# A transformer layer on one core: VectorE takes over the low parts of split queries and keys from GpSimd

## The chip, the cores and the metric

One Trainium2 chip, one core of it. The metric is the device time of one execution in microseconds; three runs of the kernel before gave a median of 1078.43 (1077.81 to 1080.08). The engines' short names in the profile are PE (TensorE), DVE (VectorE), ACT (ScalarE), POOL (GpSimd) and SP (SyncE).

## The reference, cut to what matters

Batch 8, sequence 1024, width 192, 12 heads of 16, hidden width 768, all float32.

```python
h = segm_table[seg] + pos + token_table[tok]
x = layernorm(h)
q, k, v = split(x @ qkv_weight.T)              # per head, 16 wide
q = layer_norm(q) * 16 ** -0.5                  # normalised over the 16
k = layer_norm(k)
h = h + softmax(q @ k.T) @ v @ proj_weight.T
x = layernorm(h)
xq = round(clip(x / mean(alpha_a1), -8, 7));  wq1 = round(clip(w1 / alpha_w1[:, None], -8, 7))
x1 = clip(gelu(xq @ wq1.T * alpha_w1 * mean(alpha_a1) + b1), -10, 10)
hq = round(clip(x1 / mean(alpha_a2), -8, 7)); wq2 = round(clip(w2 / alpha_w2[:, None], -8, 7))
h = h + hq @ wq2.T * alpha_w2 * mean(alpha_a2) + b2
```

## The kernel before

The 8 sequences are cut into 16 halves of 512 tokens, each of four tiles of 128 (TH = 4). The kernel runs 18 half-steps as a software pipeline: in half-step s TensorE, ScalarE and VectorE do the attention of half s, the first norm, the QKV projection and the split of queries and keys of half s + 2, the projection and the FFN's first part of half s - 1, and the FFN's end of half s - 2. Before half-step 0 a start does the work of the first halves ("half -1", "half -2" below are the passes labelled s = -1 and -2). No loop of the hardware is used; every instruction is written out.

Attention is done in 24 units a half-step (UNITS): a unit is a group of 4 heads against one tile of 128 keys. Per unit TensorE multiplies the scores (`scores`, L1073), ScalarE takes exp in two passes (`exps`, L645), and two units later TensorE multiplies by the values (`heads`, L1093), over a PSUM bank that VectorE copies out once in 8 units (`head_outputs`, L796, word `o`).

Between the units stands the other work, in an order written out by hand: PLAN (L77) has one line for a unit, START_PLAN (L128) is the same for the start and half-step 0. Every engine walks through the same list and does its part of each word, in this order; an engine's queue is never reordered. The capital words are jobs: TensorE fills one of three PSUM banks (`job`, L1097), then VectorE (or ScalarE, where START_PLAN has the small letter) copies it out (`job_result`, L819); job n + 3 in the list waits for the copy of job n. The words that matter here: B the query and key projection, r the sums of squares on VectorE, S the reciprocal roots on VectorE (`qk_roots`, a chain of 12 small linked instructions), n0 to n3 the split of one tile each (`split_qk`), D and E the transposes of the stacked queries and keys, C the values, x0 to x5 the quantising of gelu's output (`quantise_gelu`, L812, three instructions each: L815, L816, L817), Y the FFN's second matmul (L1171). Y0 waits for the last of the six `hq`. The end of a half-step's list is `S0 n0 / n1 o / D0 x0 E0 C1 / n2 C2 D1 / E1 n3 / D2 x1 / D3 E2 x2 / E3 x3 x4 / x5 C3`, and the next one begins with `o / Y0 Y1 Y2 F0 ...`.

Queries and keys go to TensorE as float16 pairs, a high part and a rest (low part), four copies of 16 columns for each head: q as high, high, low, low and k as high, low, high, low. `split_qk` makes them: one product (`sq`, L778) scales the tile by its root, then two casts write the high parts of q and k (L783). The low parts, float32 minus high, are two subtractions that GpSimd does (`split_low`, L564), each 128 x 384. `sq` and `stack` have two buffers each (t % 2). TensorE's D and E wait for `stack_ready`, which GpSimd raises. In half -2 VectorE does the low part of k itself (L789), beside GpSimd's low part of q.

GpSimd's queue in a half-step: `add_result` (the bias and the residual of the FFN, it waits for the last Y copy of VectorE), four gathers of segment rows and four of token rows for a half three ahead, the squares of four tiles (L553, for r), and at the end `split_low`. In the start the gathers of token rows of halves 2 and 3 stand behind `split_low(-2)` and `split_low(-1)`. SP issues the loads of positions and the stores.

On VectorE an instruction that reads what the one ahead wrote is linked to it by a semaphore (`link`, L670): the queue waits for its end. Instructions without a link overlap by a little.

Of the kernel before, what the change touches and what calls it, by code (L numbers as in the profile page):

```python
# [25 lines left out]
ALU = mybir.AluOpType  # L26
# [4 lines left out]
B, SEQ = 8, 1024  # L31
C = 192
H, D = 12, 16
HID = 768
TB = SEQ // P
TH = TB // 2
# [163 lines left out]
def job_half(kind, s):  # L200
    return s + LAG[kind]


def job_runs(kind, s0):
    return s0 == 1 if kind == "W" else 0 <= job_half(kind, s0) < HALVES
# [26 lines left out]
def layer(nc, x_tok, x_seg, tok_table, seg_table, w_qkv, w_proj, w1, b1, aw1, aa1, w2, b2, aw2, aa2,  # L232
          pos, out):
    ctx = ExitStack()
    with ctx:
# [3 lines left out]
        def sem(name):  # L239
            return ctx.enter_context(nc.semaphore(name))  # L240
# [31 lines left out]
        def squares_at(half0, t):  # L272
# [70 lines left out]
            sem(n) for n in ("hot_ready", "hot_mm", "hot_out", "rows_mm", "rows_added"))  # L343
        w_mm, scale_ready, high_weights, warm_ready = (
            sem(n) for n in ("w_mm", "scale_ready", "high_weights", "warm_ready"))
        hn_first, low_k_ready, squared_act = sem("hn_first"), sem("low_k_ready"), sem("squared_act")
        idx_ready, ident_ready = sem("idx_ready"), sem("ident_ready")
        pool_step, dve_step = sem("pool_step"), sem("dve_step")
        weights_ready, proj_ready = sem("weights_ready"), sem("proj_ready")
# [3 lines left out]
            sem(n) for n in ("hn_ready", "stack_ready", "xq_ready", "hq_ready"))  # L353
        scores_mm, exp_done, heads_mm, heads_out = (
            sem(n) for n in ("scores_mm", "exp_done", "heads_mm", "heads_out"))
        squared, summed, high_ready = sem("squared"), sem("summed"), sem("high_ready")
        out_ready, stored = sem("out_ready"), sem("stored")
        job_mm = {k: sem(f"{k}_mm") for k in PER_HALF}
        job_out = {k: sem(f"{k}_out") for k in PER_HALF}
# [1 line left out]
        def nth(half, t, per):  # L361

            return half * per + (t + 1)
# [56 lines left out]
        def stack_parts(t):  # L420

            for n, (high, low) in enumerate(((slice(0, 2), slice(2, 4)), (slice(0, 4, 2), slice(1, 4, 2)))):
                src = sq[:, t % 2, n * C:(n + 1) * C].rearrange("p (h d) -> p h d", d=D)
                src = src.unsqueeze(2).broadcast_to([P, H, 2, D])
                yield stack[:, t % 2, n, :, high, :], stack[:, t % 2, n, :, low, :], src
# [66 lines left out]
        def _(pool):  # L492
# [51 lines left out]
            def square(s0, s):  # L544
                if not job_runs("B", s0):
                    return
                half = job_half("B", s)
                for t in range(TH):

                    pool.wait_ge(job_out["B"], nth(half, t, TH))  # L550
                    if job_half("B", s0) > 2 or t >= 2:
                        pool.wait_ge(summed, half * TH + (t - 1))
                    nc.gpsimd.tensor_tensor(sq[:, t % 2], qk[:, t], qk[:, t], ALU.mult).then_inc(squared, 1)  # L553

            def split_low(s0, s):
                if not job_runs("D", s0):
                    return
                for t in range(TH):

                    pool.wait_ge(high_ready, nth(job_half("D", s), t, TH))  # L560
                    parts_ = list(stack_parts(t))

                    for high, low, src in parts_ if s0 > -2 else parts_[:1]:
                        last = nc.gpsimd.tensor_tensor(low, src, high, ALU.subtract)  # L564
                    last.then_inc(stack_ready, 1)

            def add_result(s0, s):
                if not job_runs("Y", s0):
# [11 lines left out]
            def one(s0, s, b):  # L580

                add_result(s0, s)
                ahead = s0 + GATHER_AHEAD
                if FIRST_GATHERED <= ahead < HALVES:
                    add_segments(ahead)
                    add_tokens(ahead)
                square(s0, s)
                split_low(s0, s)

            pool.wait_ge(idx_ready, 3)  # L590
            add_segments(2)
            add_segments(3)
            split_low(-2, -2)
            add_tokens(2)
            split_low(-1, -1)
            add_tokens(3)
            halfsteps(one)

# [68 lines left out]
        def _(dve):  # L667
# [9 lines left out]
            tt = nc.vector.tensor_tensor  # L677
# [93 lines left out]
            def split_qk(s0, s, t):  # L771

                half, h0 = job_half("D", s), job_half("D", s0)
                g = lambda a: a.rearrange("p (g d) -> p g d", d=D)
                if TH * h0 + t >= 2:

                    dve.wait_ge(stack_ready, half * TH + (t - 1))
                link(tt(g(sq[:, t % 2]), g(qk_at(h0, t)), rq[:, t, 0:GROUPS].unsqueeze(2).broadcast_to([P, GROUPS, D]), ALU.mult))  # L778
                if TH * h0 + t >= 2:

                    dve.wait_ge(job_mm["E"], half * TH + (t - 1))
                for high, low, src in stack_parts(t):
                    last = nc.vector.tensor_copy(high, src)  # L783

                last.then_inc(high_ready, 1)
                if s0 == -2:

                    dve.wait_ge(high_ready, t + 1)
                    tt(low, src, high, ALU.subtract).then_inc(low_k_ready, 1)  # L789

            def head_outputs(s0, s, p):

# [213 lines left out]
        def _(pe):  # L1006
# [90 lines left out]
            def job(s0, s, kind, t):  # L1097
# [27 lines left out]
                        last = mm(ps[:, 0:hi - lo], partsT[:, t, m], w, start=(n == 0), stop=(n == len(passes) - 1))  # L1125
                if kind in "DE":
                    pe.wait_ge(stack_ready, nth(half, t, TH))
                    if s0 == -2 and kind == "E":
                        pe.wait_ge(low_k_ready, t + 1)
                    for i in range(H // 2):  # L1130
                        src = stack[:, t % 2, "DE".index(kind), 2 * i:2 * i + 2].rearrange("p h a d -> p (h a d)")
                        last = nc.tensor.transpose(bank16((kind, t), s0, F16)[:, i * P:(i + 1) * P], src, ident_h[:])  # L1132
# [94 lines left out]
```

## Time and profile before

| | |
|---|---|
| median of three runs | 1078.43 us |
| the profiled execution | 1076.59 us |
| its span | 1074.8 us |
| mean granted TensorE clock | 0.977 of full speed |
| GpSimd's subtractions L564 | 124, 120.6 us busy |
| VectorE's casts L783 | 128, 58.7 us busy |

The busy share of an engine says how full it is over the whole span, not whether it holds the others up. The chain of waits says that: it is followed back from the last instruction, at each step to what released it. In the timeline, several instructions of one line that follow each other are one row ("x2"), from the first's start to the last's end; a number in brackets is the time that the engine was idle ahead of it, and who released it.

### The profile page before, as it was taken

How to read it: one execution, taken by the hardware profiler on the slowest of the kernel's cores; microseconds unless marked ns; L12 is line 12 of the kernel's file. 1: busy time of each engine (PE TensorE's matmuls, PEld its weight loads, DVE VectorE, ACT ScalarE, POOL GpSimd, SP SyncE). 2: the span in 40 equal slices, each digit the busy share in tenths (PEclk: the TensorE clock that was granted, in tenths of full speed). 3: DMA queues.
4: the chain of work that ended last, by engine and by line, in shares of the span. 5: the costliest groups of instructions: out<-in, count | busy, mean ns of one | idle time of the engine just before them, and what ended most of it. 6: DMA issues, size and time to landing. Idle time of an engine off the chain costs nothing.

```text
span 1074.8 us, 19548 instructions
## 1 busy us (share of the span) xinstructions
PE 978.3 (91%) x7571; PEld 387.7 (36%) x7571; DVE 814.1 (76%) x2318; ACT 867.7 (81%) x937; POOL 415.6 (39%) x347
## 2 busy tenths in 40 slices
PE   5599999999999999999999999999999999989873
PEld 4333434334343433334342433434243343413131
DVE  5978869698786969788686968878696978715265
ACT  1387798897979888898979889797988889798951
POOL 6554513536344452644444353534445314101011
PEclk9799999999999999999999999999999999989995
DMA  7510200303011030203112040201102000000000
GB/s 161 127 20 12 31 1 1 45 2 70 5 31 16 17 59 1 45 1 62 14 23 23 1 75 2 39 7 30 16 10 37 1 16 1 16 1 16 1 15 16
DMA packets 25329, 28.61 MB, mean 27 GB/s; under 512 B 4979, under 2 KB 21622, under 8 KB 25238
## 3 DMA queue, kind: packets, MB, share of 16 engines
q0 software_dynamic: 16896, 11.80, 9.3%
q1 hardware_dynamic: 8192, 15.55, 4.8%
q8 instruction: 61, 1.00, 0.4%
q14 instruction: 30, 0.25, 0.1%
q10 hardware_dynamic: 150, 0.01, 0.0%
HBM read 21.06 MB, written 6.29 MB: 25 GB/s over the span
## 4 chain that ended last, share of the span: by engine, by line
PE 40%; ACT 29%; DVE 24%; issue 3%; POOL 3%; POOLq 0%; DMA 0%; DVEq 0%
ACT probs L645 22%; PE ps_o L1093 12%; PE ps_s L1073 8%; PE ps_j L1117 4%; ACT gelu L639 4%; PE ps_j L1171 3%; POOL stack L564 3%; PE ps_j L1125 2%; PE ps_j L1132 2%; PE ps_j L1138 2%; ACT L639 2%; PE ps_j L1157 2%; ACT L645 2%; PE ps_j L1142 2%; DVE hn L734 2%
## 5 line engine op out<-in xcount | busy, mean ns | idle before, releaser
L645 ACT ACTIVATE probs<-ps_s 128x1024 f32<-128x1024 f32 x768 | 736.5, 1023 | 126.0 <-PE ps_s L1073 121.5
L1093 PE MATMUL ps_o<-probs,v_sb 128*32 128x512 f32 x3072 | 394.9, 605 | 0.2 <-DVE o_sb L796 0.2
L1073 PE MATMUL ps_s<-qT,kT 64*128 64x512 f16 x1536 | 264.1, 384 | 35.0 <-ACT probs L645 24.5
L564 POOL TENSOR_TENSOR stack<-sq,stack 128x384 f16<-128x384 f32 x124 | 120.6, 993 | 161.6 <-DVE stack L783 161.6
L1073 PEld LDWEIGHTS ps_s<-qT,kT 64*128 64x128 f16 x1536 | 61.4, 93 | 299.8 <-ACT probs L645 273.8
L573 POOL TENSOR_TENSOR y_sb<-y_sb,b_row 128x768 f32<-128x768 f32 x16 | 29.0, 1815 | 277.8 <-DVE y_sb L868 277.8
L497 POOL DMA_INDIRECT h_all<-in_L_tok_token_table,idx x60 | 96.9, 1614 | 59.1 <-DMA h_all<-in_L_tok_segm_table,idx 40.8
L1093 PEld LDWEIGHTS ps_o<-probs,v_sb 128*32 128x32 f32 x3072 | 69.1, 109 | 123.7 <-issue 115.6
L553 POOL TENSOR_TENSOR sq<-qk 128x384 f32<-128x384 f32 x56 | 46.2, 826 | 139.5 <-DVE qk L831 139.5
L497 POOL DMA_INDIRECT h_all<-in_L_tok_segm_table,idx x56 | 87.2, 1557 | 15.2 <-issue 13.7
L639 ACT ACTIVATE gelu<-ps_j,b_sb,s_sb 128x512 f32<-128x512 f32 x96 | 69.9, 773 | 26.1 <-PE ps_j L1157 25.1
L1132 PE MATMUL ps_j<-ident_h,stack 128*128 128x128 f16 x768 | 61.3, 225 | 12.3 <-POOL stack L564 10.8
L831 DVE TENSOR_SCALAR qk<-ps_j,w_back 128x384 f32<-128x384 f32 x56 | 34.6, 618 | 48.6 <-PE ps_j L1125 48.5
L1125 PE MATMUL ps_j<-wh,partsT 128*128 128x384 f16 (+1 forms) x384 | 70.4, 293 | 1.1 <-ACT partsT L626 0.7
L796 DVE COPY o_sb<-ps_o 128x512 f32<-128x512 f32 x48 | 32.7, 681 | 47.7 <-PE ps_o L1093 47.7
L1132 PEld LDWEIGHTS ps_j<-ident_h,stack 128*128 128x128 f16 x768 | 45.6, 100 | 50.7 <-issue 39.8
L815 DVE TENSOR_SCALAR gelu<-gelu,ia,qlo 128x512 f32<-128x512 f32 x96 | 61.8, 643 | 2.0 <-ACT gelu L639 2.0
L1157 PE MATMUL ps_j<-xqT,w1T 96*128 96x512 bf16 x192 | 58.4, 402 | 4.1 <-ACT gelu L639 2.5
L783 DVE CAST stack<-sq 128x384 f16<-128x384 f32 x128 | 58.7, 500 | 2.2
L816 DVE TENSOR_SCALAR gelu<-gelu,qhi 128x512 f32<-128x512 f32 x96 | 53.8, 560 | 3.4
L1125 PE MATMUL ps_j<-wl,partsT 128*128 128x192 f16 (+1 forms) x256 | 53.1, 290 | 0.0
L1117 PE MATMUL ps_j<-wpT,oT 96*128 96x192 f32 x256 | 48.7, 333 | 0.0
(148 smaller groups left out, 1089.3 us busy)
## 6 DMA issues: line engine op xcount, KB each, us to landing
out<-h_all SPq DMA_DIRECT2D x16, 384.0 KB, 2.4
h_all<-in_positions SPq DMA_DIRECT2D x7, 768.0 KB, 5.1
gelu<-in_L_ffn_w SPq DMA_DIRECT2D x2, 576.0 KB, 11.7
h_all<-in_L_tok_token_table,idx POOLq DMA_INDIRECT x60
h_all<-in_L_tok_segm_table,idx POOLq DMA_INDIRECT x56, 4.6
probs<-in_L_attn_qkv_weight SPq DMA_DIRECT2D x2, 432.0 KB, 5.4
h_all<-in_positions SPq DMA_DIRECT2D x2, 384.0 KB, 6.2
o_nat<-in_L_ffn_alpha_a SPq DMA_DIRECT2D x1, 384.0 KB, 5.0
```

Of the source, the lines that this page charges most:

```text
L497: nc.gpsimd.indirect_dma_start(out=h_tile(half, j), out_offset=None, in_=table, in_offset=bass.IndirectOffsetOnAxis(ap=idx[:, which, t:t + ...
L564: last = nc.gpsimd.tensor_tensor(low, src, high, ALU.subtract)
L639: nc.scalar.activation(gelu[:, j], bank(("X", j), s0), ACT.Gelu, bias=b1_sb[:, j:j + 1], scale=s1_sb[:, j:j + 1]).then_inc(job_out["X"], 1)
L645: nc.scalar.activation(probs[:, u % PROBS, 2 * pair:2 * pair + 2], ps_s[:, 2 * pair:2 * pair + 2], ACT.Exp, scale=SCORE_SCALE).then_inc(ex ...
L783: last = nc.vector.tensor_copy(high, src)
L815: link(ts(gelu[:, t], gelu[:, t], ia2[:], qlo[:], ALU.mult, ALU.max))
L1073: last = mm(ps_s[:, j], kT[rows, par, head // 2, m * P:(m + 1) * P], qT[rows, par, head // 2, nh * NQ:(nh + 1) * NQ], start=True, stop=True)
L1093: last = mm(ps_o[32 * j:32 * j + 2 * D, :], v_sb[:, par, m, (GH * group + j) * VE:(GH * group + j) * VE + 2 * D], probs[:, u % PROBS, j], ...
L1117: last = mm(ps[:, 0:C], oT[:, t, k], wpT[:, k], start=(k == 0), stop=(k == 1))
L1125: last = mm(ps[:, 0:hi - lo], partsT[:, t, m], w, start=(n == 0), stop=(n == len(passes) - 1))
L1132: last = nc.tensor.transpose(bank16((kind, t), s0, F16)[:, i * P:(i + 1) * P], src, ident_h[:])
L1157: last = mm(ps, w1T[:, k, t * P:(t + 1) * P], xqT[:, k], start=(k == 0), stop=(k == 1))
```

## The change

`split_low` goes from GpSimd. In `split_qk` VectorE links to its casts, then does the two subtractions of the tile and raises `stack_ready` itself, in every half. The semaphores `high_ready` and `low_k_ready` fall away. The squares of GpSimd for tiles 0 and 1 get a wait of their own on `stack_ready`, since the buffer `sq` is now read last by VectorE.

```diff
@@ -343,7 +343,7 @@
             sem(n) for n in ("hot_ready", "hot_mm", "hot_out", "rows_mm", "rows_added"))
         w_mm, scale_ready, high_weights, warm_ready = (
             sem(n) for n in ("w_mm", "scale_ready", "high_weights", "warm_ready"))
-        hn_first, low_k_ready, squared_act = sem("hn_first"), sem("low_k_ready"), sem("squared_act")
+        hn_first, squared_act = sem("hn_first"), sem("squared_act")
         idx_ready, ident_ready = sem("idx_ready"), sem("ident_ready")
         pool_step, dve_step = sem("pool_step"), sem("dve_step")
         weights_ready, proj_ready = sem("weights_ready"), sem("proj_ready")
@@ -353,7 +353,7 @@
             sem(n) for n in ("hn_ready", "stack_ready", "xq_ready", "hq_ready"))
         scores_mm, exp_done, heads_mm, heads_out = (
             sem(n) for n in ("scores_mm", "exp_done", "heads_mm", "heads_out"))
-        squared, summed, high_ready = sem("squared"), sem("summed"), sem("high_ready")
+        squared, summed = sem("squared"), sem("summed")
         out_ready, stored = sem("out_ready"), sem("stored")
         job_mm = {k: sem(f"{k}_mm") for k in PER_HALF}
         job_out = {k: sem(f"{k}_out") for k in PER_HALF}
@@ -550,19 +550,10 @@
                     pool.wait_ge(job_out["B"], nth(half, t, TH))
                     if job_half("B", s0) > 2 or t >= 2:
                         pool.wait_ge(summed, half * TH + (t - 1))
+                    if t < 2 and job_half("B", s0):
+
+                        pool.wait_ge(stack_ready, half * TH + (t - 1))
                     nc.gpsimd.tensor_tensor(sq[:, t % 2], qk[:, t], qk[:, t], ALU.mult).then_inc(squared, 1)
-
-            def split_low(s0, s):
-                if not job_runs("D", s0):
-                    return
-                for t in range(TH):
-
-                    pool.wait_ge(high_ready, nth(job_half("D", s), t, TH))
-                    parts_ = list(stack_parts(t))
-
-                    for high, low, src in parts_ if s0 > -2 else parts_[:1]:
-                        last = nc.gpsimd.tensor_tensor(low, src, high, ALU.subtract)
-                    last.then_inc(stack_ready, 1)
 
             def add_result(s0, s):
                 if not job_runs("Y", s0):
@@ -585,14 +576,11 @@
                     add_segments(ahead)
                     add_tokens(ahead)
                 square(s0, s)
-                split_low(s0, s)
 
             pool.wait_ge(idx_ready, 3)
             add_segments(2)
             add_segments(3)
-            split_low(-2, -2)
             add_tokens(2)
-            split_low(-1, -1)
             add_tokens(3)
             halfsteps(one)
 
@@ -779,14 +767,12 @@
                 if TH * h0 + t >= 2:
 
                     dve.wait_ge(job_mm["E"], half * TH + (t - 1))
+                for high, _, src in stack_parts(t):
+                    last = nc.vector.tensor_copy(high, src)
+                link(last)
                 for high, low, src in stack_parts(t):
-                    last = nc.vector.tensor_copy(high, src)
-
-                last.then_inc(high_ready, 1)
-                if s0 == -2:
-
-                    dve.wait_ge(high_ready, t + 1)
-                    tt(low, src, high, ALU.subtract).then_inc(low_k_ready, 1)
+                    last = tt(low, src, high, ALU.subtract)
+                last.then_inc(stack_ready, 1)
 
             def head_outputs(s0, s, p):
 
@@ -1125,8 +1111,6 @@
                         last = mm(ps[:, 0:hi - lo], partsT[:, t, m], w, start=(n == 0), stop=(n == len(passes) - 1))
                 if kind in "DE":
                     pe.wait_ge(stack_ready, nth(half, t, TH))
-                    if s0 == -2 and kind == "E":
-                        pe.wait_ge(low_k_ready, t + 1)
                     for i in range(H // 2):
                         src = stack[:, t % 2, "DE".index(kind), 2 * i:2 * i + 2].rearrange("p h a d -> p (h a d)")
                         last = nc.tensor.transpose(bank16((kind, t), s0, F16)[:, i * P:(i + 1) * P], src, ident_h[:])
```

## Rows read from the trace of the kernel before

**Rows 1.** Page, part 1: busy us, share of span, instructions

```profile
PE 978.3 (91%) x7571; PEld 387.7 (36%) x7571; DVE 814.1 (76%) x2318; ACT 867.7 (81%) x937; POOL 415.6 (39%) x347
```

**Rows 2.** Chain of waits, half-step 13: start us, us, what

```profile
907.66 1.81 POOL stack L564 x2
909.46 0.14 issue
909.60 0.50 PE ps_j L1132 x6
...
920.76 1.59 PE ps_j L1171 x18
```

**Rows 3.** Single lines, whole span: ns min/median/max, first and last start

```profile
L564 POOL TENSOR_TENSOR stack<-sq,stack x124: 910/922/1287, 42.4 to 911.5; 128x384 f16<-128x384 f32 x124
...
L789 DVE TENSOR_TENSOR stack<-sq,stack x4: 557/559/559, 42.4 to 49.7; 128x384 f16<-128x384 f32 x4
...
L778 DVE TENSOR_TENSOR sq<-qk,rq x60: 548/557/1159, 65.1 to 908.8; 128x384 f32<-128x384 f32 x60
...
L778 DVE TENSOR_TENSOR sq<-probs,rq x4: 557/762/1265, 41.1 to 48.2; 128x384 f32<-128x384 f32 x4
...
L815 DVE TENSOR_SCALAR gelu<-gelu,ia,qlo x96: 537/542/951, 165.1 to 1062.7; 128x512 f32<-128x512 f32 x96
...
L816 DVE TENSOR_SCALAR gelu<-gelu,qhi x96: 485/486/1033, 166.1 to 1063.3; 128x512 f32<-128x512 f32 x96
```

**Rows 4.** Timeline of VectorE, half-step 13: start us, us, instructions

```profile
899.43 0.63 DVE L783 CAST stack<-sq 128x384 f16<-128x384 f32 x2
899.98 0.55 DVE L778 TENSOR_TENSOR sq<-qk,rq 128x384 f32<-128x384 f32 x1
900.56 1.96 DVE L783 CAST stack<-sq 128x384 f16<-128x384 f32 x2
902.44 0.68 DVE L796 COPY o_sb<-ps_o 128x512 f32<-128x512 f32 x1
903.26 0.56 DVE L833 COPY qT<-ps_j 128x768 f16<-128x768 f16 x1
...
920.10 0.43 DVE L817 TENSOR_SCALAR hq<-gelu 128x512 bf16<-128x512 f32 x1
```

**Rows 5.** 13 stretches ahead of Y0, VectorE: L783, L815, L778, L816 in turn

```profile
sum 280.54, DVE 49.94; mean DVE 3.84
...
sum 280.54, DVE 52.02; mean DVE 4.00
...
sum 280.54, DVE 36.08; mean DVE 2.77
...
sum 280.54, DVE 44.71; mean DVE 3.44
```

**Rows 6.** Timeline of GpSimd, half-step 13

```profile
900.14 2.16 POOL L564 TENSOR_TENSOR stack<-sq,stack 128x384 f16<-128x384 f32 x2 [5.29 <-DVE stack L783]
...
923.69 1.81 POOL L573 TENSOR_TENSOR y_sb<-y_sb,b_row 128x768 f32<-128x768 f32 x1 [11.10 <-DVE y_sb L868]
```

**Rows 7.** Timeline of TensorE: first and last of 13 Y0

```profile
182.10 1.66 PE L1171 MATMUL ps_j<-w2T,hq 128*128 128x192 bf16 x18
...
920.70 1.66 PE L1171 MATMUL ps_j<-w2T,hq 128*128 128x192 bf16 x18
```

**Rows 8.** VectorE from 61 to 83 us: L778, then L783

```profile
61.00:83.00 22.00, 3.41 (x4) 1.00 0.09 12
...
61.00:83.00 22.00, 3.12 (x8) 1.00 0.09 12
```

**Rows 9.** Timelines of the start: TensorE, VectorE, TensorE

```profile
82.75 0.33 PE L1145 MATMUL ps_j<-ident_h,parts 128*128 128x128 f16 x3 [1.04 <-DVE parts L738]
...
100.99 0.56 DVE L833 COPY qT<-ps_j 128x768 f16<-128x768 f16 x1 [1.44 <-PE ps_j L1132]
...
120.13 0.84 PE L1138 MATMUL ps_j<-ident,o_sb 128*128 128x128 f32 x6 [1.38 <-DVE o_sb L800]
```

## The prediction

> **What bounds the kernel now.** I read the page's busy shares first. TensorE is busy 91% of the span, ScalarE 81%, VectorE 76%, GpSimd 39% [rows 1]. No single share decides, so I followed one half-step in the chain of waits, in order of time. There GpSimd appears once: the two low-part subtractions of the third tile, 1.81 us, and behind them six transposes of TensorE [rows 2]. That looks like a wait that the change removes. The chain then runs on TensorE to the second FFN matmul (job Y0, L1171) at 920.76. The question is who else has to be ready at Y0.
>
> Y0 waits for the last `hq` of `quantise_gelu`, on VectorE. That instruction starts at 920.10 and takes 0.43, so it ends at 920.53 [rows 4]. A wait of TensorE on another engine takes 0.14 to be seen (the "issue" piece at 909.46) [rows 2], so Y0 could start at 920.67; it starts at 920.70 [rows 7]. VectorE has 0.03 us of slack at Y0. The timeline shows the same gap of 0.17 +- 0.01 at all 13 Y0 from 182.10 to 920.70, 61.54 us apart [rows 7]. TensorE and VectorE arrive there together: whatever lengthens VectorE's queue between the roots (S0) and the last `hq` (x5) moves Y0.
>
> In that stretch VectorE never rests, but for one place: the copy L796 starts at 902.44 and takes 0.68; an instruction without a wait starts some 0.08 before the end of the one ahead (casts 899.43 + 0.63, next at 899.98), so the queue is free at 903.04 and the qT copy starts at 903.26 [rows 4]. Idle: 0.22 us.
>
> **The change part by part.** (1) Added to VectorE, per tile (4 in a half-step): a wait between casts and subtractions, and two subtractions. The casts now run to their end (0.63 instead of 0.55 in the queue) and the link costs 0.03, as between all linked instructions (the product of 899.98, 0.55 long, ends at 900.53 and its casts start at 900.56) [rows 4]: +0.11. The subtraction has been on VectorE four times, in the prologue, for the key half: 557 to 559 ns, even beside GpSimd's own [rows 3]; less the overlap of 0.08 that is 0.48 in the queue, two are 0.96. Sum 1.07 a tile, 4.28 a half-step. The query form (other stride on the low part) is not shown on VectorE: from above the bound is 1.16 us, what the product L778 takes at worst [rows 3] (beside GpSimd, which won't be busy), from below 0.35, the second cast of a pair (0.63 less the 0.28 after which it starts is about that; the cast has one input less). I take 0.56, the row of the same operation.
>
> (2) Removed from VectorE: the slowing by GpSimd's subtractions. The second tile's casts take 1.96 where the first tile's take 0.63, and GpSimd runs two subtractions from 900.14 to 902.30 beside them [rows 4, 6]. The sums per half-step over the 13 stretches [rows 5] against the median, undisturbed durations [rows 3]: casts 3.84 against 4 x 0.63, so 1.32; L815 4.00 against 6 x 0.542, 0.75; L778 2.77 against 4 x 0.557, 0.54; L816 3.44 against 6 x 0.486, 0.52. Together 3.13. Copies from PSUM are not slower beside GpSimd (qT 0.56) [rows 4] and give nothing.
>
> The Trainium skill ("SBUF — State Buffer", Who interferes with whom) gives a reason: the second pair of SBUF ports is locked for a whole instruction by GpSimd or by a VectorE cast, copy or tensor_scalar in its double rate, and a VectorE instruction with two SBUF inputs fights with GpSimd's reads. This rule speaks against the change in one point: the new subtractions have two SBUF inputs and would be exposed themselves, so with any GpSimd instruction left beside them the sum would be larger, by up to that instruction's length. GpSimd has none left there (it is idle for 5.29 us ahead of its first subtraction and for 11.10 behind its last) [rows 6], so the sum stays; in the prologue, the one place where the two run side by side, VectorE's stayed at 557 to 559 [rows 3] and the trace does not bear the rule out.
>
> (3) Net for VectorE up to the last `hq`: 4.28 - 3.13 = +1.15; the idle 0.22 and the slack 0.03 take their share: Y0 moves by 0.90 us. TensorE meanwhile gains: the third tile's parts are ready 0.03 + 1.04 behind the casts instead of 1.81 and a hand-over [rows 2], but VectorE comes to that tile 0.2 later (+1.07 twice, less 1.33 at the casts, 0.22 idle and 0.40 at the first slow L815); my estimate is that the transposes start 0.3 earlier. TensorE then waits at Y0, so the gain is lost. After Y0 the chain is on TensorE's own queue [rows 2], with no slack that the move could vanish in: scores, heads, the projection, then the norm. 13 x 0.90 = 11.7.
>
> (4) The start. In the stretch 61 to 83 (half -1) four tiles are split: +4.28; L778 sums to 3.41 against 4 x 0.557 (-1.18), the casts to 3.12 against 2.52 (-0.60) [rows 8]: +2.5. TensorE waits there for VectorE's `parts`, 1.04 us at 82.75 [rows 9], so it comes through whole. In half 0 the first tiles' part vanishes: VectorE waits 1.44 us for TensorE at 100.99 [rows 9], more than two tiles add with some slowing gone, and again ahead of the third. The fourth tile's 1.07 comes out: TensorE waits 1.38 for L800 behind it, at 120.13 [rows 9]. In half -2 one subtraction a tile is added, 4 x 0.48 = 1.9, against the slowing of the four products there (median 762 and worst 1265, against 557) [rows 3], which is 1.1, and of what comes behind them: +0.4. Together 4.0; its bounds are 0 (VectorE has gaps that I can't place) and 2 x 4.28 + 1.9, near 10.
>
> (5) GpSimd's queue: 124 subtractions of 0.92 us at best leave [rows 3]. Four token gathers each of halves 2 and 3, which stood behind them, are issued earlier; earlier can only help who reads them: 0. Squares wait in steady halves for VectorE's copy and will still: 0. The new wait (square of tile 0 or 1 on `stack_ready` of the previous half) asks for the third and fourth tile of the half before, split a half-step (61.54 us) less some 20 ahead of it: 0. `add_result` waits 11.10 us for VectorE's y_sb [rows 6], so an empty queue does not bring it forward; DMA issues behind it stay where they are relative to it: 0. Behind the new link on VectorE stands everything up to x5; that is the cost above.
>
> Sum: 11.7 + 4.0 = 15.7 us on the profiled run's 1076.59 (its span 1074.8 and 1.8 around it), so 1092.3. The median of the three runs is 1078.43, 1.84 above the profiled run; with the same distance 1094.1. I predict 1094 us, slower by 1.5%.
>
> **The rivals.** *Faster* (8%): the slack at Y0 is VectorE's and not a tie, or a subtraction is cheaper. Then what counts is the one GpSimd piece on the chain. It decides from the point where eight subtractions are 0.90 cheaper together, 0.45 us each instead of 0.56. TensorE then gets its third tile's transposes 0.3 earlier each half-step: 13 x 0.3 = 4, so 1074.5. For it: the 1.81 us in the chain; against: four rows within 2 ns.
>
> The Trainium skill ("GPSIMD Engine Reference", Engine selection) sends elementwise work on a tile to VectorE, GpSimd being about twice slower for two inputs; here it is 0.92 against 0.56, 1.65 times [rows 3]. By it the move pays; that is this rival, and what it leaves out is whose queue is full.
>
> *Absorbed* (9%): Y0 moves, but a ScalarE run later in the half-step hides it (exp passes fill 81% of the engine) [rows 1], and only the start's 4 us or less comes through: between 1078.4 and 1083, say 1081. Against it: the chain behind 920.76 is TensorE's, not ScalarE's [rows 2].
>
> *The slowing stays* (4%): slow casts are VectorE's own, not due to GpSimd. Then 4.28 - 0.25 = 4.0 passes 13 times, and at the start up to 10: some 60 us, 1138. Against it: slow instructions stand beside GpSimd's and only there.
>
> *The change relieves nothing* because GpSimd's next work moves into the stretch and slows VectorE again (2%): at most 3.13 x 13 = 41 us more, 1135. Nothing is ready for it: GpSimd's next piece waits 11.10 us [rows 6].
>
> **How the numbers follow.** My forecast has 77%. Its own range: 0.90 is a difference of 4.28 and 3.13, each good to some 0.25, so 0.55 to 1.25 a half-step, 13 times that is 7 to 16; the start 1.5 to 6: 1087 to 1100. For the 8 in 10 I reach down into the absorbed case, to 1080, and up to 1100. Less than 0.2% (2.2 us) can't be told from no change here. Faster by more than that: 0.07. Within: 0.06 (the rest of the first rival, the lower end of the absorbed one). Slower: 0.87.
>
> **What would show it.** In the changed kernel's profile: cast pairs of 0.63 in every tile, and L815, L816 without slow ones (step 2); pairs of subtractions on VectorE of 1.04 us from first start to last end (step 1); VectorE busy 814 + 124 x 0.56 less the slowing, near 840; GpSimd near 415.6 - 120.6 = 295; a half-step of 62.4 instead of 61.54, read between Y0 starts; TensorE idle at Y0 by 0.8 to 1.2 with VectorE's `hq` as releaser (step 3); TensorE's wait at 82.75 longer by 2.5 (step 4). If the half-step is 61.2 and the transposes' wait is all that changed, the rival of a faster kernel is right. If Y0 moves and the half-step does not grow, it was absorbed.

## The result: 1.55% slower, and the profile after

The changed kernel takes 1096.31 us (median of 4 runs, 1092.76 to 1097.26) against 1078.32 (4 runs) before: ratio 1.0155, 95% interval 1.0136 to 1.0175 (the quotient of the two medians is 1.0167). The forecast was 1094. The profiled execution took 1095.96, 19.4 more than that of the kernel before, of which the sum had named 15.7.

The page of the changed kernel answers to [rows 1]; behind it the row of the subtractions, now VectorE's, with the mean duration in ns:

```profile
PE 983.0 (90%) x7571; PEld 392.4 (36%) x7571; DVE 829.4 (76%) x2442; ACT 867.6 (79%) x937; POOL 294.4 (27%) x223
...
L774 DVE TENSOR_TENSOR stack<-sq,stack 128x384 f16<-128x384 f32 x128 | 65.7, 555 | 2.2
```

GpSimd lost 121.2 us of work, VectorE's busy time grew by 15.3 only: 124 subtractions were added, some 69 us. Of that 44.0 came back, because the products, the casts and the first two quantising instructions became shorter (together 216.3 before, 172.3 now); most of the rest is the overlap of some 0.08 between neighbours in the queue, which busy time counts once. The single lines of the changed kernel show it (ns min/median/max; product, cast, first and second quantising instruction), against [rows 3]:

```profile
L766 DVE TENSOR_TENSOR sq<-qk,rq x60: 546/549/561, 66.9 to 928.1; 128x384 f32<-128x384 f32 x60
...
L771 DVE CAST stack<-sq x128: 341/359/539, 42.1 to 929.0; 128x384 f16<-128x384 f32 x128
...
L801 DVE TENSOR_SCALAR gelu<-gelu,ia,qlo x96: 535/540/546, 174.7 to 1081.6; 128x512 f32<-128x512 f32 x96
...
L802 DVE TENSOR_SCALAR gelu<-gelu,qhi x96: 485/486/490, 175.3 to 1082.2; 128x512 f32<-128x512 f32 x96
```

The long ones are gone: the worst product was 1159, the worst L815 (now L801) 951. Still the kernel is slower. TensorE's timeline says where, at the first and the last of the 13 Y0 [rows 7]; the brackets are the time that TensorE was idle ahead, and for whom:

```profile
191.85 1.31 PE L1155 MATMUL ps_j<-w2T,hq 128*128 128x192 bf16 x14 [0.90 <-DVE hq L803]
...
939.58 1.65 PE L1155 MATMUL ps_j<-w2T,hq 128*128 128x192 bf16 x18 [0.91 <-DVE hq L803]
```

Three things are to be seen. The first Y0 is 9.75 us later than before (182.10), the last 18.88 (920.70), so 12 half-steps cost 9.13, 0.76 each (most are 62.3 to 62.4 long, 61.54 to 61.63 before). And at each Y0 TensorE now waits 0.90 for the last `hq`, where the kernel before shows no wait. Behind the last Y0 nothing more is lost up to the kernel's last FFN matmuls (1083.27 - 939.58 = 143.69, and 1064.39 - 920.70 = 143.69).

One half-step of VectorE in the changed kernel, against [rows 4]: tile 0's and tile 1's casts with the subtractions behind them, the copy L782, the qT copy, and the end of the queue.

```profile
668.54 0.63 DVE L771 CAST stack<-sq 128x384 f16<-128x384 f32 x2
...
670.16 0.55 DVE L766 TENSOR_TENSOR sq<-qk,rq 128x384 f32<-128x384 f32 x1
670.74 0.63 DVE L771 CAST stack<-sq 128x384 f16<-128x384 f32 x2
671.40 1.03 DVE L774 TENSOR_TENSOR stack<-sq,stack 128x384 f16<-128x384 f32 x2
672.35 0.68 DVE L782 COPY o_sb<-ps_o 128x512 f32<-128x512 f32 x1
672.95 0.55 DVE L819 COPY qT<-ps_j 128x768 f16<-128x768 f16 x1
...
689.99 0.43 DVE L803 TENSOR_SCALAR hq<-gelu 128x512 bf16<-128x512 f32 x1
```

From the first tile's casts to the second's product there are now 1.62 us (668.54 to 670.16), 0.55 before (899.43 to 899.98): 1.07 as worked out. The second tile's casts take 0.63, not 1.96. The idle time ahead of qT is gone. `hq` ends at 690.42, TensorE starts at 690.57. In the chain of waits no other engine stands between the product at 667.95 and Y0, only VectorE and its "issue" pieces; the chain's last pieces:

```profile
690.43 0.14 issue
690.57 0.49 PE ps_j L1155 x4
```

### The profile page after: what moved, and what is told of

It is laid out like the page before. It is cut to its first block, busy times and chain, and to the rows that moved or that the text cites. A ratio compares the mean times of both kernels' runs of the same rounds, so it can differ in the third digit from the quotient of the medians.

```text
span 1094.1 us, 19550 instructions
## 1 busy us (share of the span) xinstructions
PE 983.0 (90%) x7571; PEld 392.4 (36%) x7571; DVE 829.4 (76%) x2442; ACT 867.6 (79%) x937; POOL 294.4 (27%) x223
## 4 chain that ended last, share of the span: by engine, by line
DVE 49%; PE 31%; ACT 14%; issue 5%; POOL 1%; POOLq 0%; DMA 0%; DVEq 0%
ACT probs L633 10%; PE ps_o L1079 6%; DVE stack L774 5%; PE ps_s L1059 4%; PE ps_j L1103 4%; DVE gelu L802 4%; DVE stack L771 4%; DVE gelu L801 4%; PE ps_j L1155 3%; PE ps_j L1111 3%; DVE hq L803 3%; DVE sq L766 3%; DVE kT L819 3%; DVE qT L819 2%; PE ps_j L1141 2%
## 5 line engine op out<-in xcount | busy, mean ns | idle before, releaser
L782 DVE COPY o_sb<-ps_o 128x512 f32<-128x512 f32 x48 | 32.7, 682 | 47.7 <-PE ps_o L1079 47.7
L774 DVE TENSOR_TENSOR stack<-sq,stack 128x384 f16<-128x384 f32 x128 | 65.7, 555 | 2.2
L1116 PEld LDWEIGHTS ps_j<-ident_h,stack 128*128 128x128 f16 x768 | 45.3, 100 | 46.8 <-issue 39.9
L1155 PE MATMUL ps_j<-w2T,hq 128*128 128x192 bf16 x384 | 38.6, 253 | 16.8 <-DVE hq L803 16.8
L801 DVE TENSOR_SCALAR gelu<-gelu,ia,qlo 128x512 f32<-128x512 f32 x96 | 51.8, 539 | 2.0 <-ACT gelu L627 2.0
L802 DVE TENSOR_SCALAR gelu<-gelu,qhi 128x512 f32<-128x512 f32 x96 | 46.7, 486 | 3.4
```

What stands on the lines that cost most here:

```text
L774: last = tt(low, src, high, ALU.subtract)
L801: link(ts(gelu[:, t], gelu[:, t], ia2[:], qlo[:], ALU.mult, ALU.max))
L802: link(ts(gelu[:, t], gelu[:, t], qhi[:], ROUND, ALU.min, ALU.add))
L1155: last = mm(ps[:, 0:C], hq[:, j, t * P:(t + 1) * P], w2T[:, j], start=(j == 0), stop=(j == HB - 1))
```

## The experiments

The stretch that the change works in can be measured directly in every trace: from the start of tile 0's product (at the end of S0) to the end of the last `hq` on VectorE, and to Y0 on TensorE. Each number below varies by at most 0.04 over the 12 half-steps behind the first Y0 (the lighter kernel is one of the experiments below); the stretch from Y0 to that product is 39.2 to 39.9 in all of them.

| kernel | to the end of `hq` | to Y0 |
|---|---|---|
| before | 21.68 | 21.86 |
| changed | 22.47 | 22.61 |
| tile 0 on VectorE | 21.41 | 21.59 |
| tile 2 on VectorE | 22.15 | 22.33 |
| one more subtraction | 22.93 | 23.07 |
| lighter | 20.89 | 21.63 |
| GpSimd's work beside | 26.23 | 26.37 |

The theory, from here on: the half-step is set at Y0, where TensorE and the end of VectorE's queue from S0 to x5 meet; that queue holds its own work and what GpSimd slows of it. Its rivals: the GpSimd piece on the chain is what counts; the slow instructions have another cause; the whole loss lies in the start. Four experiments use one form of the kernel in which each tile's low parts belong to either engine (with a semaphore of its own for VectorE's tiles); the condition is the one of the first line or one of those in the comments:

```diff
+        def on_dve(g):
+            s0, t = g // TH - 2, g % TH
+            return s0 <= 0                     # start only
+            # s0 > 0                            steady half-steps only
+            # s0 > 0 and t == 0                 tile 0
+            # s0 > 0 and t == 2                 tile 2
...
-                    pool.wait_ge(high_ready, nth(job_half("D", s), t, TH))
+                    if on_dve(job_half("D", s) * TH + t):
+                        continue
+                    pool.wait_ge(high_ready, pool_tiles(nth(job_half("D", s), t, TH)))
```

### The start alone, the steady half-steps alone

> VectorE does the low parts in the start and half-step 0 only (halves -2, -1, 0); from half-step 1 on GpSimd does them as before. Theory (a full VectorE queue in every half-step, and in the start the same plus a TensorE clock that falls after longer waits): first Y0 about 9.0 us later than before (191.1 instead of 182.1), half-steps of 61.54 behind it, in all 1078.3 + 9.0 = 1087. The granted clock falls to 0.5 for a few us behind the waits of TensorE near 86 and 128 us. Rival (the start costs only its added VectorE work, the clock has nothing to do with it): 4.6 us, 1083. Rival (the whole loss is in the steady half-steps): 1078 to 1080.

> VectorE does the low parts from half-step 1 on only (13 times); the start is as before. Theory: start unchanged, first Y0 at 182.1 + 0.8 = 182.9, half-steps of 62.35, TensorE idle for 0.90 at each Y0; in all 1078.3 + 13 x 0.8 = 1088.7. Rival (what the start lost made the steady loss too, through the order in which engines meet): half-steps back near 61.54 and 1078 to 1081. The sum of the gains of this run and of the one with the start only should be the whole change, 18 us; if it is much less, the two losses share a cause.

Measured on one chip, the kernel before at 1077.75: start only 1084.64 (ratio 1.0058, 1.0042 to 1.0074), steady only 1087.76 (1.0097, 1.0081 to 1.0112). The losses of 6.9 and 10.0 add up to 16.9 of the 18.0: they are two, and nearly independent. The timelines of TensorE, first and last Y0, of the start only and then of the steady half-steps only:

```profile
192.28 1.66 PE L1196 MATMUL ps_j<-w2T,hq 128*128 128x192 bf16 x18
...
931.28 1.66 PE L1196 MATMUL ps_j<-w2T,hq 128*128 128x192 bf16 x18
```

```profile
183.65 1.65 PE L1196 MATMUL ps_j<-w2T,hq 128*128 128x192 bf16 x18 [0.91 <-DVE hq L842]
...
931.04 1.65 PE L1196 MATMUL ps_j<-w2T,hq 128*128 128x192 bf16 x18 [0.90 <-DVE hq L842]
```

With the start changed, 739.0 us lie between the two (before: 738.6) and TensorE does not wait at Y0; with the steady part changed, 747.4 and 0.90 of waiting. The start-only median fell 2.4 short of the expected 1087; the rival's 1083, without a part for the clock, is nearer. Its profiled run had the first Y0 10.2 late, but 1.6 of that was there before the first split instruction (42.74 against 41.11), and its four runs lie in two pairs, near 1083 and near 1086. The medians leave the size of the start's second part open; the clock, below, bears on it.

### Tile 0, tile 2

> From half-step 1 on VectorE does the low parts of tile 0 of each half, GpSimd those of tiles 1 to 3. Theory (what counts is the length of VectorE's queue from S0 to x5, own work plus slowing by GpSimd): tile 0 adds 1.07 and takes away the slowing of tile 1's casts, 1.33, so the queue is 0.26 shorter in each half-step, and TensorE gets the third tile's parts as much earlier; half-step 61.3, in all 1075 to 1078. Rival (GpSimd's slowing is small beside the added work, each tile moved costs its 1.07 less idle): half-step 62.4, 1089. Rival (a quarter of the change gives a quarter of the loss): +0.2 a half-step, 1081.

> From half-step 1 on VectorE does the low parts of tile 2 alone, the tile whose two GpSimd subtractions stood on the chain of waits of the kernel before; GpSimd does tiles 0, 1 and 3. Theory (length of VectorE's queue): +1.07, and the slowing of the product of tile 3 goes, -0.57, so +0.50 a half-step, Y0 later by as much less 0.03: 13 x 0.47 = 6, in all 1084. Rival (the piece on the chain is what counts): transposes of tile 2 start 0.3 earlier or more, half-step 61.2, 1074 to 1076, and better than with tile 0 moved.

Tile 0 on VectorE: 1074.06, ratio 0.9964 (0.9950 to 0.9978), faster than both kernels; a half-step is (917.92 - 182.28) / 12 = 61.30. Tile 2, the one whose GpSimd piece stood on the chain [rows 2]: 1084.36, ratio 1.0060 (1.0043 to 1.0076), and 62.06 a half-step. The first and last Y0, of tile 0 and then of tile 2:

```profile
182.28 1.66 PE L1196 MATMUL ps_j<-w2T,hq 128*128 128x192 bf16 x18
...
917.92 1.66 PE L1196 MATMUL ps_j<-w2T,hq 128*128 128x192 bf16 x18
```

```profile
183.51 1.66 PE L1196 MATMUL ps_j<-w2T,hq 128*128 128x192 bf16 x18
...
928.23 1.66 PE L1196 MATMUL ps_j<-w2T,hq 128*128 128x192 bf16 x18
```

The same edit on two tiles has opposite signs, as the difference of added work and removed slowing has: tile 0 adds 1.07 and frees tile 1's casts of 1.33; tile 2 adds 1.07 and frees 0.57. VectorE's stretch in the table moves by -0.27 and +0.47. That the piece on the chain decides is refuted.

Yet TensorE does not wait at Y0 in either run, although VectorE's `hq` came 0.47 later in the second. The reason stands in the kernel before and was overlooked: TensorE's side of the meeting point also hangs on VectorE's queue, through GpSimd's low parts of the fourth tile (tile 3). GpSimd's two subtractions of that tile, TensorE's transposes behind them (D3 and E2), and the same transposes with tile 2 on VectorE:

```profile
910.61 1.99 POOL L564 TENSOR_TENSOR stack<-sq,stack 128x384 f16<-128x384 f32 x2 [1.16 <-DVE stack L783]
```

```profile
912.74 0.83 PE L1132 MATMUL ps_j<-ident_h,stack 128*128 128x128 f16 x12
```

```profile
920.27 0.83 PE L1157 MATMUL ps_j<-ident_h,stack 128*128 128x128 f16 x12 [0.82 <-POOL stack L583]
```

In all 13 half-steps of the kernel before D3 starts 0.14 or 0.15 behind the end of GpSimd's work, and Y0 follows 7.95 or 7.96 later; with tile 0 or tile 2 on VectorE it is the same, and with tile 2 there TensorE waits 0.82 ahead of D3. So both sides of the tie start at VectorE's casts of tile 3: one is VectorE's own rest of the queue, the other GpSimd's 1.99 and TensorE's 7.96, and it comes 0.03 later. What lengthens VectorE's queue ahead of that point moves both. The chain of [rows 2] named GpSimd's piece of tile 2; the one that held TensorE was that of tile 3. Tile 3 alone on VectorE was not run.

In the timeline of the tile 0 mixture, VectorE ahead and GpSimd behind, the reason why tile 1 may stay on GpSimd can be seen: its two subtractions run beside two copies from PSUM, which keep their 0.69 and 0.56, and touch L840 only at their end (0.68, undisturbed 0.54). Tile 1's casts take 0.63 here and 1.96 in the kernel before, with GpSimd's work of tile 0 gone from beside them.

```profile
654.17 0.63 DVE L802 CAST stack<-sq 128x384 f16<-128x384 f32 x2
654.72 0.69 DVE L821 COPY o_sb<-ps_o 128x512 f32<-128x512 f32 x1
655.80 0.56 DVE L858 COPY qT<-ps_j 128x768 f16<-128x768 f16 x1 [0.40 <-PE ps_j L1157]
656.28 0.68 DVE L840 TENSOR_SCALAR gelu<-gelu,ia,qlo 128x512 f32<-128x512 f32 x1
```

```profile
654.88 1.79 POOL L583 TENSOR_TENSOR stack<-sq,stack 128x384 f16<-128x384 f32 x2 [7.49 <-DVE stack L802]
```

### GpSimd's work put back beside VectorE's

```diff
+                if s0 > 0 and job_runs("D", s0):
+                    for t in range(TH):
+                        pool.wait_ge(high_ready, (s0 - 1) * TH + t + 1)
...
+                        for n in range(2):
...
+                            nc.gpsimd.tensor_tensor(junk[:, 2 * t + n], a, c, ALU.subtract).then_inc(junk_done, 1)
...
+                if s0 > 0:
+                    nc.vector.memset(gate_sb[:], 0.0).then_inc(high_ready, 1)
```

> The changed kernel, and from half-step 1 on GpSimd does two subtractions of 128 x 384 per tile again, of constants into a buffer that nobody reads, released by a small VectorE memset between the casts and the subtractions; nobody waits for them. They add only GpSimd work beside VectorE's (and four memsets of 0.06). Theory (GpSimd's subtractions slow VectorE's casts, products and tensor_scalars that run beside them): casts, L815, L816 and products are slow again here and there, half-step longer by 1 to 3 us than 62.35, in all 1110 to 1135. Rival (the slow instructions of the kernel before had another cause, as the wait for GpSimd's result): +0.06 x 4 x 13 = 3 us, 1099.

Measured: 1142.72 (ratio to the kernel before 1.0602, 1.0583 to 1.0622), 46 more than the changed kernel and above the expected range. Nobody waits for this work, and the small memset that releases it lies within a subtraction's time, so what it costs is slowing: 3.7 us a half-step (66.03). The timeline of VectorE, then that of GpSimd:

```profile
634.39 1.26 DVE L778 TENSOR_TENSOR sq<-qk,rq 128x384 f32<-128x384 f32 x1
635.69 0.63 DVE L783 CAST stack<-sq 128x384 f16<-128x384 f32 x2
636.36 0.55 DVE L788 TENSOR_TENSOR stack<-sq,stack 128x384 f16<-128x384 f32 x1
636.38 0.06 DVE L786 MEMSET gate_sb<- 128x1 f32 x1
636.83 1.27 DVE L788 TENSOR_TENSOR stack<-sq,stack 128x384 f16<-128x384 f32 x1
638.02 0.68 DVE L796 COPY o_sb<-ps_o 128x512 f32<-128x512 f32 x1
```

```profile
636.52 2.35 POOL L590 TENSOR_TENSOR junk<-b_row,wh 128x384 f16<-128x384 f32 x2 [1.28 <-DVE gate_sb L786]
```

The first subtraction, ahead of GpSimd's, keeps 0.55; the second, which comes while GpSimd's first is on, takes 1.27; the copy from PSUM keeps 0.68. Four times 0.72, 0.71 at one product and 0.14 at one L815 are 3.7. I had priced only the casts, products and tensor_scalars behind the subtractions and not the subtractions themselves, which are the dearest of all here. That is what the Trainium skill's rule on the shared ports ("SBUF — State Buffer", Who interferes with whom) says of an instruction with two SBUF inputs: who comes second waits for the other. The prediction had read the prologue's four rows as not bearing it out; they were all of the first kind, ahead of GpSimd's, and it was GpSimd's that took longer there (the maximum of 1287 in [rows 3]). The second kind stood in the same rows: the product has two SBUF inputs too, and beside GpSimd it took up to 1265 in the prologue and 1159 later; in this run, with no GpSimd work beside the prologue's products, they are back at 547 to 557.

The run does not bring back everything: no cast is slowed in it (the longest takes 0.56) and no second quantising instruction (0.49), because GpSimd's work lies beside others. For the casts the evidence is tile 1 of the mixture above.

### Longer and shorter queue

```diff
+                if s0 > 0 and t == TH - 1:
+                    high, _, src = next(iter(stack_parts(t)))
+                    tt(junk[:], src, high, ALU.subtract)
```

> The changed kernel, with one more subtraction of 128 x 384 on VectorE in tile 3 of each half from half-step 1 on, into a buffer that nobody reads. Theory (VectorE's queue sets Y0, one for one): +0.48 in each of 13 half-steps, 6.2 us, 1096.3 + 6 = 1102.5, TensorE's wait at Y0 1.38 instead of 0.90. Rival (the queue has slack somewhere behind Y0 that takes part of it): less than 3 us.

```diff
-                link(ts(gelu[:, t], gelu[:, t], qhi[:], ROUND, ALU.min, ALU.add))
+                if s0 <= 1 or t < 3:
+                    link(ts(gelu[:, t], gelu[:, t], qhi[:], ROUND, ALU.min, ALU.add))
```

> The changed kernel without the second of the three quantising instructions (min and add) for three of the six blocks x3, x4, x5 from half-step 2 on: VectorE's queue is 3 x 0.52 = 1.56 shorter ahead of Y0; the result lacks that clip and rounding in half of the hidden columns. Theory (a tie: TensorE's own work is only 0.90 behind): TensorE's wait at Y0 goes and with it 0.9 of a half-step, not 1.56; 12 x 0.9 = 11 and 1.5 at the end, where this work stands alone, so 1084. Rival (VectorE alone sets the half-step): 12 x 1.56 + 1.5 = 20, 1076.

One more: 1100.50, 4.2 above the changed kernel. Lighter, which leaves out the clip and rounding of half the hidden columns and so computes another result: 1080.93, 15.4 below it. First and last Y0 of one more, then of the lighter one:

```profile
190.11 1.65 PE L1159 MATMUL ps_j<-w2T,hq 128*128 128x192 bf16 x18 [1.03 <-DVE hq L807]
...
943.86 1.65 PE L1159 MATMUL ps_j<-w2T,hq 128*128 128x192 bf16 x18 [1.03 <-DVE hq L807]
```

```profile
188.93 1.65 PE L1156 MATMUL ps_j<-w2T,hq 128*128 128x192 bf16 x18 [0.89 <-DVE hq L804]
...
925.20 1.66 PE L1156 MATMUL ps_j<-w2T,hq 128*128 128x192 bf16 x18
```

Between first and last Y0: 753.75 with one more, 747.73 in the changed kernel, so 0.50 in each of 12 half-steps for the 0.48 added, one for one. TensorE's wait at Y0 grew only to 1.03, not to 1.38, because it now waits ahead of D3 as well:

```profile
934.80 0.83 PE L1120 MATMUL ps_j<-ident_h,stack 128*128 128x128 f16 x12 [0.29 <-DVE stack L778]
```

With 1.58 less in the queue Y0 to Y0 is 736.27: 0.95 a half-step less, and the wait is gone from the second Y0 on; `hq` is ready 0.74 ahead of Y0. Beyond that, shortening this end of VectorE's queue gives nothing, because TensorE's side is the next bound: 21.63 from tile 0's product to Y0, against 22.61 with VectorE's side last. That is TensorE's side of the tie in the changed kernel. (The first Y0 came 1.7 and 2.9 us earlier than in the profiled run of the changed kernel, in kernels whose start is the same; that is most of what the medians have below 6 and above 12.6, the latter being 11.46 between the first and the last Y0 and 1.15 behind it.)

### The clock in the start

```diff
+                fill = {("A", -1): 14, ("A", 0): 20, ("F", 1): 30}.get((kind, s0), 0) if t == 0 else 0
+                for _ in range(fill):
+                    nc.tensor.transpose(bank16((kind, t), s0, F16)[:, 0:P], ident_h[:], ident_h[:])
```

The stretches of the changed kernel (busy time and number of instructions of each engine, then the granted clock, 0.58 and 0.61) and, in the second fence, those of the same work in the filled kernel:

```profile
88.00:92.00 4.00, 4.00 (x19) 2.12 (x17) 1.96 (x6) 1.14 (x2) 0.90 (x2) 0.58 0.00 0
128.00:132.00 4.00, 4.00 (x22) 3.30 (x21) 2.78 (x9) 1.94 (x2) 0.00 (x0) 0.61 0.00 0
```

```profile
84.00:88.00 4.00, 4.00 (x42) 2.63 (x40) 2.94 (x8) 1.94 (x2) 0.63 (x1) 1.00 0.00 0
124.00:128.00 4.00, 3.84 (x28) 2.54 (x28) 3.02 (x12) 1.94 (x2) 0.00 (x0) 1.00 0.00 0
```

> The changed kernel with transposes of the identity on TensorE, whose result is overwritten, ahead of three waits of the start: 14 ahead of the transposes of half 1's norm (near 54 us), 20 ahead of those of half 2 (near 86), 30 ahead of F0 of half 0 (near 128). They fit into waits of 2.0, 1.7 and 2.6 us. Theory (TensorE's clock falls to half behind those waits, and the matmuls at half clock cost 4.4 us in three places): granted clock 1.0 from 57 us on, 3 to 4.4 us less: 1092 to 1093. Rival (the lower clock has nothing to do with the idle time ahead of it): clock as in the changed kernel, 1096 to 1097.

Measured: 1092.70, 3.6 less than the changed kernel, by instructions that compute nothing; its first Y0 is at 186.91 instead of 191.85, and the half-steps are the same 62.3. The four runs go from 1091.29 to 1094.77, and the lowest of the changed kernel, 1092.76, lies among them; the two ratios, 1.0141 and 1.0155, have overlapping intervals, so the size of the gain is uncertain. In the changed kernel TensorE runs at half clock (1.2 GHz) for a few us behind a wait of 1.68 (at 86.51) and again behind one of 2.56 (at 127.74); with these waits filled it stays at 2.4 there. The kernel before had waits of 1.04 and 1.38 there [rows 9] and no such drop.

The filled kernel was to be at full clock from 57 us on, and was not: the clock fell once, behind a wait that had not been filled. The same wait is in the changed kernel, which stayed at full clock behind it (the filled kernel first; the second line of each fence is one microsecond behind the wait, with the granted clock, 0.50 and 1.00, third from the end):

```profile
73.21 1.92 PE L1079 MATMUL ps_o<-probs,v_sb 128*32 128x512 f32 x8 [2.03 <-DVE o_sb L782]
...
74.00:75.00 1.00, 1.00 (x8) 0.00 (x0) 0.96 (x4) 0.00 (x0) 0.00 (x0) 0.50 0.00 0
```

```profile
75.77 1.07 PE L1079 MATMUL ps_o<-probs,v_sb 128*32 128x512 f32 x8 [2.08 <-DVE o_sb L782]
...
76.00:77.00 1.00, 1.00 (x11) 0.12 (x4) 1.00 (x3) 0.00 (x0) 0.00 (x0) 1.00 0.00 0
```

So the length of a wait alone does not decide. The kernels with one more subtraction and with less in the queue have the same start as the changed one; in them the clock fell behind this wait (2.05 and 2.03) and not near 86, where their wait was 0.37 and 0.42. With the start only and with GpSimd's work beside it stayed full behind this wait (2.09 and 2.08). And with GpSimd's work beside, TensorE waits 1.45 for the copy of `o_sb`, and 0.79 soon after, in the same place of all 13 half-steps; the clock fell behind two of them.

One of the four runs of the changed kernel, 1092.76, had a mean clock of 0.975 instead of the 0.971 of the three others; it has no trace that would say where.

### The faster version, with and without filling

> The faster mixture (from half-step 1 on VectorE does the low parts of tile 0, GpSimd those of tiles 1 to 3), with 14 transposes of the identity on TensorE ahead of its wait for half 1's norm near 54 us, overwritten afterwards. In the mixture's trace the clock is at 0.5 until 57 us and the work between 54 and 57 runs at half speed. Theory: the clock rises before the real transposes, 1 us less, 1073. Rival: the clock rises when it does, whatever runs ahead of 54 us, 1074 or, if the filling holds up the transposes, 1075.

> The mixture without the filling, again, beside it on the same chip: 1074, half-step 61.27, 0.3 to 0.4% below the kernel before.

With filling 1075.03 (0.9966, 0.9954 to 0.9978), without 1074.68 (0.9969, 0.9957 to 0.9981): no difference. The tile 0 mixture holds its gain, 3.6 us, in a second measurement. Why a clock that was full from 55 us on (in the unfilled run from 59.9) brought nothing to the median stays open. The profiled run with filling was already 2.5 us late at its first split instruction (43.64 against 41.16); from there to the first Y0 it took 139.90, the two unfilled runs of this kernel 140.82 and 141.95.

## Why the prediction was right

**Y0 as the meeting point, and the tie.** Right: one more and lighter show both sides of it. What the prediction did not see is why the two sides arrive together: both hang on VectorE's casts of tile 3, TensorE's through GpSimd. It took the 0.03 for VectorE's slack against work of TensorE's own. For the whole change this made little difference, since VectorE's side became the later one.

**The price in the queue (step 1).** 1.07 a tile, measured 1.07. The query form costs the same as the key form (548 to 560 ns over all 128). VectorE's busy time was to be near 840 and is 829.4: the sign left out the overlap of 0.08 that step 1 itself takes off, some 10 us over 124 subtractions.

**The slowing (step 2).** All of it went, as the four lines show. That its cause is GpSimd's work, and not a coincidence of place, is shown for products and the first quantising instruction by the run that puts the work back, and for the casts by the mixture with tile 0. For the second quantising instruction it rests on the place alone.

**What passes (step 3).** 13 x 0.90 = 11.7 was forecast. Measured: 9.13 for 12 half-steps and about 0.8 in the first, 9.9 in all. This term was mis-sized: VectorE's stretch grew by 0.79 where 4.28 - 3.13 - 0.22 = 0.93 was worked out, the terms being together 0.14 off, and Y0 moved by 0.75 or 0.76. That TensorE's wait is 0.90, the number forecast for the move, is a coincidence: the wait is the move of 0.75 and some 0.15 by which TensorE's side got shorter. The prediction had 0.3 for the latter.

**The start (step 4).** This term was mis-sized: 4.0 was forecast, 8.9 came in the profiled run. Read off the two timelines, the delay is 0.44 at half 1's norm transposes (forecast 0.4), and grows by 1.38 until the first product of half -1, 1.94 until half 2's norm transposes (forecast 2.5), 1.60 until half 0's first product, 2.25 until F0 (forecast 1.1), 1.39 until the FFN's first matmuls (157.44, before 148.45), and 0.75 until the first Y0. The first piece agrees by luck: 0.40 of its 0.44 was there before the first split instruction (41.51 against 41.11). The second, fourth and sixth, 4.4 together, hold no added VectorE work; in each of them TensorE's clock was late in rising (full from 60.6 us, from 56.9 before) or fell behind a wait. No step had asked what a longer wait does to the clock; the granted clock of the kernel before was at full in these places. In half 0 more than the fourth tile's 1.07 came out: 0.91 by the third tile's product and 0.27 more by the fourth's. The sign of step 4 was not met either: the wait at 82.75 became 1.68 at 86.51, 0.64 longer and not 2.5, since a wait of 2.08 at 75.77 had taken a part.

How much of the start is the change's own? From the first split instruction to the first Y0 the kernel before takes 140.99. The change adds, with what the first steady half-step adds taken off, 8.5 to 8.6 in the profiled runs of the start only and the changed kernel, 6.3 and 5.8 in those of one more and lighter, and 4.2 when filled. The two with less had the clock at full from 57 to 58 us, the others from 61. But the late rise is no effect of the change alone: the mixture with tile 0, whose start is that of the kernel before, had it at 57.4 in one profiled run and at 59.9 in the other. So 8.9 is near the upper end of what this start costs, and the share of the clock in the medians is known only roughly, by the 3.6 of the filled kernel.

**The rivals.** Faster: refuted for the whole change. Its 1074.5 is near what tile 0 alone gives, but not by its mechanism, which was the one GpSimd piece on the chain: the move of a tile pays where the slowing that it removes is more than the 1.07 that it adds. Absorbed: refuted, 0.50 of 0.48 passes. The slowing stays, and GpSimd's next work moving in: did not happen; the run with the work put back, at 1142.72, shows what it would have cost.

The two misses, a start 4.9 too small and steady half-steps 1.8 too large, cancel in part: the profiled run was forecast at 1092.3 and took 1095.96. Another 1.5 went by luck: the forecast added the 1.84 by which the median before lay above its profiled run, and for the changed kernel that distance is 0.35. So 1094 against 1096.3 is nearer than the parts deserve.

## What to carry to other kernels

Where two engines meet at one instruction, look for who else arrives within a few hundredths of a microsecond, and follow both sides back to where they part; the engine of the longest piece on the chain can be relieved without gain while the other's queue grows. Price a move between VectorE and GpSimd piece by piece: what it adds to the queue against what it frees of slowing, tile by tile, since one piece can pay where the whole does not (1074.1 against 1096.3 here). And where a change lengthens a wait of TensorE, read the granted clock behind it, in more than one execution.

## What the runs showed of the hardware

- A two-input VectorE subtraction that starts while a GpSimd subtraction is on takes 1.27 us instead of 0.55; one that starts ahead of it keeps 0.55, and GpSimd's takes longer. Copies from PSUM beside the same GpSimd work keep their duration (0.68).
- Two VectorE casts of 128 x 384 (float32 to float16) take 0.63 us together, and 1.96 beside two GpSimd subtractions.
- TensorE's granted clock fell to half for a few us behind waits of 1.68 and 2.56 us and not behind 1.04 and 1.38; behind a wait of 2.0 to 2.1 in the same place it fell in three profiled runs (2.03, 2.03, 2.05) and not in three others (2.08, 2.08, 2.09), and behind 13 equal pairs of waits (1.45 and 0.79) it fell twice. 50 transposes whose result nobody uses in the first two waits, and 14 in an earlier one, took the median from 1096.3 to 1092.7.
